# State stage of a Macaron + Mamba + MoE block: half of the odd states' products with C go from VectorE to GpSimd

## The reference, cut to what matters

```
deltaA = exp(einsum('bld,dn->lbdn', delta, A))
dBu    = einsum('bld,bln,bld->lbdn', delta, Bm, x_conv)
def step(h, inp):
    dA, dbu, c = inp
    h = dA * h + dbu
    y = einsum('bdn,bn->bd', h, c)      # sum over the 16 states of h * C
    return (h, y)
_, ys = lax.scan(step, h0, (deltaA, dBu, C_t))
y = ys + x_conv * D
y = y * silu(z)
```

## Time and profile before

| | us |
|---|---|
| median of 3 executions | 938.44 |
| the three | 932.56, 938.44, 939.86 |
| span of the profiled execution, first to last instruction | 936.1 |
| state stage in it, 540 to 804 | 264 |

### The profile page before, as it was taken

The page is one execution under the profiler, slowest core; times in us unless marked ns, Lnnn a source line. Parts: engine busy times, 40 slices in busy tenths (PEclk is TensorE's granted clock), DMA queues, the critical chain, the costliest instruction groups (busy, mean ns, idle before and its releaser), DMA issues. The chain is left out here.

```text
span 936.1 us, 11120 instructions
## 1 busy us (share of the span) xinstructions
PE 713.1 (76%) x3706; PEld 492.4 (53%) x3706; DVE 592.4 (63%) x1012; ACT 371.6 (40%) x754; POOL 347.5 (37%) x422
## 2 busy tenths in 40 slices
PE   3887887889885987599248578888778879675990
PEld 2766453444333766488146345545445545564880
DVE  6868445767522776344367686788988798662333
ACT  4411334255563322033124844586544444130330
POOL 3223222201112202536310055566656667124462
PEclk9989677779888895899769679999999999867995
DMA  4945622020001910364400000000051000103435
GB/s 179 284 62 94 82 36 37 2 35 2 1 1 55 392 35 13 122 184 165 146 1 0 1 0 1 1 1 1 1 216 54 1 0 1 35 24 129 129 123 174
DMA packets 37640, 65.98 MB, mean 70 GB/s; under 512 B 11618, under 2 KB 27618, under 8 KB 35954
## 3 DMA queue, kind: packets, MB, share of 16 engines
q1 hardware_dynamic: 33074, 52.89, 20.1%
q0 software_dynamic: 4512, 12.39, 3.7%
HBM read 39.65 MB, written 21.69 MB: 66 GB/s over the span
## 5 line engine op out<-in xcount | busy, mean ns | idle before, releaser
L1260 PE MATMUL PS<-FB,C 128*128 128x512 f32 x256 | 134.5, 621 | 4.2 <-DVE FB L1919 3.8
L1360 ACT ACTIVATE FA<-PS 128x512 f32<-128x512 f32 (+3 forms) x192 | 80.7, 496 | 71.5 <-PE PS L1030 71.1
L2045 POOL TENSOR_TENSOR FB<-FB,RBF 128x512 f32<-128x512 f32 x51 | 65.8, 1289 | 81.8 <-DVE FB L1910 81.8
L489 PE MATMUL PS<-C,FB 128*128 128x128 f32 x250 | 45.3, 305 | 57.2 <-DVE FB L1574 30.8
L1996 POOL TENSOR_SCALAR_AFFINE_SELECT FA<-FA 128x128 f32<-128x128 f32 x128 | 36.4, 295 | 129.1 <-ACT FA L1360 126.9
L2026 POOL DMA_INDIRECT GY<-FB x62 | 60.7, 979 | 53.7 <-issue 27.5
L1642 DVE TENSOR_REDUCE FA<-PS 128x2 f32<-128x1024 f32 (+2 forms) x64 | 68.0, 1086 | 19.6 <-PE PS L1009 19.4
L489 PEld LDWEIGHTS PS<-C,FB 128*128 128x128 f32 x250 | 35.6, 158 | 68.5 <-DVE FB L1574 30.9
L1030 PE MATMUL PS<-RA 64*128 64x512 f32 (+3 forms) x192 | 60.2, 496 | 5.4 <-ACT FA L1360 4.9
L1153 PE MATMUL PS<-WE,FB 128*128 x248 | 61.0, 390 | 0.0
L2036 POOL TENSOR_TENSOR FB<-WE,FB 128x512 f32<-128x512 f32 x32 | 42.4, 1325 | 49.3 <-ACT FB L1468 49.3
(11 more groups left out here) (265 smaller groups left out, 1628.1 us busy)
## 6 DMA issues: line engine op xcount, KB each, us to landing
WE<-in_wr SPq DMA_DIRECT2D x8, 1536.0 KB, 11.3
FB<-GX SPq DMA_DIRECT2D x14, 520.0 KB
RA<-RA SPq DMA_DIRECT2D x48, 128.0 KB, 4.8
FB<-GY SPq DMA_DIRECT2D x8, 512.0 KB, 5.7
GX<-GX SPq DMA_DIRECT2D x1, 4030.0 KB, 27.6
GX<-FA SPq DMA_DIRECT2D x1, 3968.0 KB, 16.7
FA<-in_w SPq DMA_DIRECT2D x2, 1024.0 KB, 7.0
FA<-in_qkvo SPq DMA_DIRECT2D x1, 1536.0 KB, 20.6
```

Of the source, the lines that this page charges most:

```text
L489: return pe.matmul(out, in_, ident, start=True, stop=True, is_transpose=True)
L1260: pe.matmul(bank(m), ident, shc[k % 4], start=n == 0, stop=n == DN - 1).then_inc(*yad.inc(ch, n, m))
L1360: act.activation(PT[n % 12][:, c0:], bank(ring_bank[(x, *a)])[:, c0:], ACT.Exp, scale=0.25).then_inc(*exd.inc(*a))
L2045: pool.tensor_tensor(shc[k % 4], sh[k % 5], Cs[(stc.no[ch, n] - 1) % 2], ALU.mult).then_inc(*cma.inc(ch, n, m))
```

## The change

Of the four products with C of an odd state, those of m = 0 and m = 2 (u = 1 and u = 5) are done by GpSimd; m = 1 and m = 3 stay on VectorE. GpSimd can't read the spread C from bank 6, so it is also spread into bank 7 and copied to SBUF, into a new tile `CO`, at u = 7 of the pair before. `bringC` stays.

```diff
-    yield [("spB", 0, 1), ("stB", 0, 1), ("spC", 0, 0), ("stC", 0, 0), ("dg", 0, 0), ...
+    yield [("spB", 0, 1), ("stB", 0, 1), ("spC", 0, 0), ("stC", 0, 0), ("spC", 0, 1), ("stC", 0, 1), ("dg", 0, 0), ...
+def on_pool(n, m):
+    return n % 2 == 0 or m % 2 == 0
...
+        if u == 7 and k < n_units and k // 8 + 1 < len(pairs):
+            c2, up = pairs[k // 8 + 1]
+            out += [("spC", c2, up + 1), ("stC", c2, up + 1)]
         yield out
...
+        CO = sb("CO", [P, CH], F)
...
+        def spread_c(n):
+            return Cs[2] if n % 2 else Cs[n // 2 % 2]
...
-        Cs = [inw.take(CH) for _ in range(2)]
+        Cs = [inw.take(CH) for _ in range(2)] + [CO[:, :]]
...
# ScalarE, stC
                     act.wait_ge(*spc.at(ch, n))
-                    if k > 1:
-                        act.wait_ge(*cma.at(*of("stC")[k - 2], 3))
-                    act.activation(Cs[k % 2], bank7("spC", ch, n), ACT.Copy).then_inc(*stc.inc(ch, n))
+                    if n % 2:
+                        if ch or n > 1:
+                            act.wait_ge(*cma.at(*((ch, n - 2) if n > 1 else (0, DN - 1)), 2))
+                    elif ch or n > 2:
+                        act.wait_ge(*cma.at(*((ch, n - 4) if n > 2 else (0, DN - 4 + n)), 3))
+                    act.activation(spread_c(n), bank7("spC", ch, n), ACT.Copy).then_inc(*stc.inc(ch, n))
# VectorE
-                elif x == "cm" and a[1] % 2:
+                elif x == "cm" and not on_pool(*a[1:]):
...
-                    if m == 0:
+                    if m == 1:
                         dve.wait_ge(*brc.at(ch, n))
# GpSimd
-                elif x == "cm" and a[1] % 2 == 0:
+                elif x == "cm" and on_pool(*a[1:]):
...
-                    pool.tensor_tensor(shc[k % 4], sh[k % 5], Cs[(stc.no[ch, n] - 1) % 2], ALU.mult).then_inc(*cma.inc(ch, n, m))
+                    pool.tensor_tensor(shc[k % 4], sh[k % 5], spread_c(n), ALU.mult).then_inc(*cma.inc(ch, n, m))
```

More of the change, by code:

```diff
@@ L349, in enter_alone @@
     yield [("dta", 0, 3), ("btx", 0)] + conv(1, 1, 1) + [("dte", 0, m) for m in range(4)] + conv(1, 1, 2, 3) + [("dtl", 0)]
-    yield [("spB", 0, 1), ("stB", 0, 1), ("spC", 0, 0), ("stC", 0, 0), ("dg", 0, 0), ("silu", 1, 0), ("silu", 1, 1)]
+    yield [("spB", 0, 1), ("stB", 0, 1), ("spC", 0, 0), ("stC", 0, 0), ("spC", 0, 1), ("stC", 0, 1), ("dg", 0, 0), ("silu", 1, 0), ("silu", 1, 1)]
     for m in range(4):
@@ L609, in build @@
         dgd = sig("s_diag", of("dg"))
-        spc, stc = sig("s_cspread_even", of("spC")), sig("s_cstore", of("stC"))
-        brc = sig("s_cspread_odd", of("bringC"))
+        spc, stc = sig("s_cspread_pool", of("spC")), sig("s_cstore", of("stC"))
+        brc = sig("s_cspread_dve", of("bringC"))
         ead, scd = sig("s_ea", of("ea")), sig("s_scan", of("scan"))
         pbd, bmd = sig("s_b_pe", of("pb")), sig("s_b_pool", of("bm"))
-        cma, cmb_ = [sig(f"s_cm{j}", [k for k in of("cm") if k[1] % 2 == j]) for j in range(2)]
+        cma, cmb_ = [sig(f"s_cm_{w}", [k for k in of("cm") if on_pool(*k[1:]) == (w == "pool")]) for w in ("pool", "dve")]
         kpd = sig("s_keep", of("keep"))
@@ L618, in cmd @@
         def cmd(ch, n, m):
-            return (cmb_ if n % 2 else cma).at(ch, n, m)
+            return (cma if on_pool(n, m) else cmb_).at(ch, n, m)
+        def spread_c(n):
+            return Cs[2] if n % 2 else Cs[n // 2 % 2]
         gth, gtl = sig("s_gate_hi", of("ghi")), sig("s_gate", of("glo"))
@@ L1285, in build @@
         fills = [x[:-1] if x[0] in ("xdt", "xbc", "mo") else x for x in plan if x[0] in after7 and (x[0] not in ("xdt", "xbc", "mo") or x[-1] == 0)]
-        early7 = [x for x in fills if x[1] == 0 and (x[0] in ("xdt", "xbc", "dt", "trb", "tru") or x in (("spB", 0, 1), ("spC", 0, 0)))]
+        early7 = [x for x in fills if x[1] == 0 and (x[0] in ("xdt", "xbc", "dt", "trb", "tru") or x in (("spB", 0, 1), ("spC", 0, 0), ("spC", 0, 1)))]
         ring7 = [x for x in fills if x not in early7 and x[0] not in ("xn",)]
@@ L1470, in scalar_program @@
                     ch, n = a
-                    k = stc.no[ch, n] - 1
                     act.wait_ge(*spc.at(ch, n))
-                    if k > 1:
-                        act.wait_ge(*cma.at(*of("stC")[k - 2], 3))
-                    act.activation(Cs[k % 2], bank7("spC", ch, n), ACT.Copy).then_inc(*stc.inc(ch, n))
+                    if n % 2:
[4 more added lines that the diff above has]
+                    act.activation(spread_c(n), bank7("spC", ch, n), ACT.Copy).then_inc(*stc.inc(ch, n))
                 elif x == "dg":
```

## The result

The changed kernel takes 953.92 us (median of 4, 953.68 to 956.12) where the kernel before took 938.5 beside it: a ratio of 1.0195, with a 95% interval of 1.0158 to 1.0231. That is some 15 to 18 us slower; I had forecast 6, and the range ended at 953. The span of the profiled execution went from 936.1 to 952.4 us.

The account below looks back on a forecast made before the run. VectorE, busy 85% of the state stage, was taken as the bound, with TensorE at 81% behind it. 3.4 + 1.8 + 1.9 + 0.5 - 3.1 + 1.5 = +6.0 us on 938.4 gave 944.4 us, range 934 to 953.

Parts of the forecast that it names:

- VectorE's relief can't be all won, TensorE stands behind it: State stage: 32 products leaving VectorE are worth 18.6 us, but TensorE's floor lets at most 0.23 us per two units through.
- E2: VectorE's scan of u = 2 in a pair of states; idle time ahead of it was to take up delays.
- E4: VectorE's scan of u = 4 in a pair of states; forecast to come 0.23 us earlier.
- the step-size pairs: Two pairs ending with a step-size tile: odd spread waits until `dta` ends; 0.96 us each, +1.9 us.
- O5 to O7 is 3.92 us, in the pairs that were tight: Scans of u = 5 to u = 7, chained over GpSimd: 3.92 us against 2.84, +3.4 us in four pairs.
- E6: VectorE's scan of u = 6 in a pair of states; the product of u = 5 stood behind it, 0.58 us.
- The spread holds `ea` of E0': Copy of the odd spread delays `ea` and the next pair's first scan: +1.8 us in six pairs, +1.9 in two.
- at the entry: Ahead of the stage's first scan: `stC` ahead of `dg` pushes ScalarE's work by 0.48 us, +0.5 us.
- side effect, +1.5: VectorE steps with two SBUF inputs stretch beside GpSimd products: two or three more at 0.6 us, +1.5 us.
- -3.1 for VectorE's side work: Six pairs where VectorE has side work and is the bound: removed products win 0.5 us on the mean, -3.1 us.
- Rival B: Ten to 15 more collisions of GpSimd products with VectorE's SBUF side steps: 952 to 957 us, chance 0.24.
- The sign: Whole kernel: the change makes it slower, by +6.0 us; slower by over 1% had chance 0.27.

Follow-up runs that it names:

- the kernel that changes nothing else: The changed kernel with the matmul of `spB` issued four times, more TensorE work ahead of `bringC`: ratio 1.0188 to the kernel before.
- the kernel with both edits: The changed kernel with `bm` one unit earlier and the odd spread at u = 1 of its own pair: ratio 0.9961 to the kernel before.
- the last kernel: The changed kernel with m = 1 and 3 on GpSimd, `bm` two units earlier, `stC` copying from bank 6: ratio 0.9828 to the kernel before.

## Why the prediction was wrong, step by step

- *VectorE's relief can't be all won, TensorE stands behind it:* right. E2 to E4 went from 2.85 to 2.61 and 2.62 in the step-size pairs, the floor named. (That all of VectorE's idle time stands ahead of an E was a little too wide: 1.0 us stands ahead of L1886 and L1873. Nothing hangs on it.)
- *O5 to O7 is 3.92 us, in the pairs that were tight:* right to 0.02, and the hand-over from GpSimd is 0.08. Where O7 alone decides it cost 0.89, 1.10 and 1.07 between E6 and E0'; forecast 1.08, in four pairs. The fourth is the norm's pair, below.
- *The spread holds `ea` of E0':* right in kind. Beside `mo` 0.17 where I had 0.28; in the step-size pairs 1.2 per pair, with the win at E4 taken off, where I had 0.96; at the entry 0.48 from `stB` to the first scan (10.33 to 10.81), as said.
- *A place missed in the same step:* I checked what empties bank 7 ahead of the new spread only for `dta`. In the norm's pair it is VectorE's L1595 behind O7, and this pair lost 2.9 where I had 0.85.
- *The term "side effect, +1.5":* mis-sized. The longer two-input steps came to 4.6 us. The price of one was right (I had 0.6, it was 0.65 on the mean), the number of them was not: seven more, not two or three. (Of the four stretched before, L1879 had been stretched by 0.65 only, from the 0.42 that it takes in the kernel after.) The sum also took -3.1 for VectorE's side work; those are the same pairs, and the collisions came to as much as the 4.5 us that were won in the whole stage. I had written that GpSimd's new product starts as the gates run, and then priced it from how seldom they collide today. The Trainium skill, GPSIMD Engine Reference, section Key points, names VectorE instructions in a 2-port mode or with two SBUF inputs as those that contend with GpSimd. For the two inputs these traces agree, since scans and products with PSUM kept their 1.21 to 1.28 and 0.66 us. One-input steps stretched too: in the kernel before, a cast beside a GpSimd product (L1516 at 547.25) took 1.14 us instead of 0.40; no run here shows which mode it ran in.
- *A term that was missing:* TensorE's clock. A later E0' lengthens the idle time ahead of `bringC` to 1.9 us and more, and in three pairs the clock fell, at 1.5 to 1.65 us each, 4.8 in all; in a fourth it fell behind the wait of the odd spread, at 0.6. The prediction took TensorE's times as constants and so had this at nothing, without a reason.

Of the 9.1 us between +6.0 and the stage's +15.1, the clock is 5.4, the collisions 3.1 and the norm's pair 2.1; the other terms leave -1.5. That these pairs lost to the clock is shown by the 0.50 in their rows. That the longer idle time is what lets it fall is shown pair by pair, in the kernels in which the idle was shortened and the full clock came back; it is not enough by itself, since waits as long kept the full clock elsewhere, and in the times it is not shown, since the kernel that changes nothing else couldn't be told from the changed one.

Rival B (collisions decide) named 952 to 957 us, and 953.9 lies in it, but by luck: it asked for ten more collisions, there were seven, worth 4.6 of the 15.1 us. And collisions about as costly, 3.7 us, stay in the kernel with both edits, which is faster than before. The sign was right in the forecast too, for waits that are there as described; it was short by the three terms above.

## What to carry to other kernels

Moving work to an engine with room cost here by its place in that engine's order more than by its duration: look for the instruction that ends up behind it and for who waits for that one; here, issuing `bm` one unit earlier and making the spread elsewhere turned +1.95% into -0.4% with the same work. When a step is added to a shared buffer, go through every user ahead of it in the list, not only the ones of a typical period. And before choosing which of equal pieces to move, ask which of them somebody waits for: the piece that held `bringC` gave 1.5% once its spread no longer went through bank 7 and `bm` stood early enough, and 0.3 to 0.5% as long as it did; the pieces moved first gave 0.4% at best. Last, a wait that gets 1 us longer can cost 1.5 us more behind it, if the clock falls in it.

## What the runs showed of the hardware

- When a GpSimd product and a VectorE step with two SBUF inputs meet, VectorE's step takes up to 1.78 us instead of 0.69 in the changed kernel, and GpSimd's up to 1.75 instead of 1.29. In the last kernel (no second spread, m = 1 and 3) such a step took 2.75 us, with two GpSimd products beside it. A cast with one SBUF input was stretched as well, from 0.40 to 1.14. Scans and products with an input in PSUM kept their time, 1.28 and 0.68 us at most in all traces.
- TensorE's granted clock fell to its lower level after 1.9 to 2.4 us of idle that had been 1.1 to 1.4, and the next `pb` and `ya` cost 1.5 us more together. It doesn't always fall: 2.37 us in the kernel before, 2.18 in the changed one and 3.21 with `bm` one unit earlier kept the full clock. The falls fell on other pairs from kernel to kernel.
- The hand-over from GpSimd to VectorE, not to be seen before, is 0.08 us, the same as the other way.
